# A graph network and mixture-of-experts kernel: late chunks of 31, 31 and 18 tiles instead of 18 and 30, and a new order around both ends of layer 2

## The chip, the cores and the metric

One core of one Trainium2 chip. The time is the device time of one execution in microseconds (us). The number to forecast is the median of the kernel's runs. Five engines work side by side: TensorE (PE, with its weight loads as PEld), VectorE (DVE), ScalarE (ACT), GpSimd (POOL) and SyncE (SP). SP, ACT and POOL also issue DMAs.

## What is computed

Two graph convolutions over 6250 nodes and 206250 weighted edges, sorted by destination, then a mixture of 8 experts, 2 chosen for each node. With rows of 256 features:

```python
norm = edge_weight * rsqrt(deg_out[src] * deg_in[dst] + EPS)
h6 = relu(segment_sum((LN(x) @ W6)[src] * norm, dst) + b6)
h7 = relu(segment_sum((h6 @ W7)[src] * norm, dst) + b7)
x = x + h7 @ Wp + bp
x = x + moe(LN(x))      # LN again, router, top 2 of 8, gelu(xn @ W1[e] + b1[e]) @ W2[e] + b2[e]
```

## The kernel before

**Two ways to sum the edges.** The sorted edges lie in tiles of 128, and 8 tiles are a group. There are 202 groups. The first edges are taken densely. A chunk of 30 or 31 tiles covers at most 128 destination rows, and for it a matrix of 128 columns by 49 x 128 source rows is built once, in layer 1. DVE makes two one-hots for a tile (`tile_one_hots`), PE multiplies them (`build_tile`, three bf16 matmuls), and DVE adds the product to the chunk's matrix in `adj` (`add_tile`). PE then multiplies the 49 blocks of the matrix with the node table in `xp` (`apply_step`; 49 blocks in 27 steps). The finished matrix is stored to `chunks` in HBM, and layer 2 only loads it (`load_chunk`, seven DMAs on ACT's queue) and applies it. The other edges are taken sparsely: POOL gathers the source rows of a group from the table in HBM with eight indirect DMAs (`gathers`), PE sums them with 16 short matmuls (`sums`) and joins every two groups (`combine`), ACT copies the result out (`copy_rows`), and SP stores it to `zsum`. Four buffers hold gathered groups (`RING`): POOL may start on a group when PE has summed the one four before.

**Layer 1** has 24 dense chunks (736 tiles) and 110 groups. The first 96 groups run beside the chunks in a loop over tiles. The last 14 (`TAIL`) have a turn each, numbered k = 0 to 13. In turns 0 to 3 PE applies the last chunk. In all of them late tiles (`EXTRAS`) are built into two further chunks, 24 and 25, of 18 and 30 tiles, which only layer 2 applies: it has 26 chunks (784 tiles), and so 104 groups. From turn 4 on the pairs 9 to 22 go through (`TAIL_PAIRS`). A pair is 256 destination rows: SP loads its sums (`load_early`), DVE scales them, PE turns them, ACT applies the relu, PE projects with W7, ACT copies out and SP stores the rows to table 1 (`store_table`). In the last turn pair 23 is projected ahead of the sums of the last group; pair 24 (the last) follows behind the last group. Chunk 24 is stored by ACT at turn 5, layer 2's chunk 0 is loaded by ACT at turn 7 into the buffer that chunk 24 left, and chunk 25 is stored by SP behind the last pair. Layer 2's gathers wait on POOL until all 25 pairs are in table 1 (`p_stored`).

**Layer 2** runs in slots, one group in each, as every engine's `layer2_slot`. A chunk spans 3 slots (chunks 0 to 7) or 4 (8 to 25), so the chunks end with slot 95 (`CHUNKS_END` = 96). A pair goes through six stages in six slots from the slot where it starts (`pair_starts`; at least three slots between starts). Stage 0 loads, scales and turns. In stage 1 PE projects with Wp and DVE adds the residual and computes two norms (`residual_and_norms`). Stage 2 is the router, stage 3 the ranks and places, stages 4 and 5 the lists of rows by expert. Pairs 0 to 10 need dense sums only, pair 11 is the merged one, and 12 to 24 need groups. At slot 96 ACT waits for the last chunk and issues 16 weight loads (`load_experts`). At slot 99 DVE works out the table of whole blocks (`list_whole`), and at slot 101 it copies the list and the first rows (`copy_list`, `block_rows`). From slot 104 on two expert blocks of 128 rows take the place of a group. Slots 104 to 112 still hold stages of the last pairs; after them come 87 blocks alone, of 105.

Before layer 1, a set-up of some 360 us computes degrees, features and bounds.

The plans follow from the constants. Starts of pairs before, as (slot, pair): (10, 0) (13, 12) (16, 1) (20, 13) (23, 2) (30, 14) (33, 3) (38, 15) (41, 4) (46, 16) (49, 5) (54, 17) (57, 6) (62, 18) (65, 7) (70, 19) (73, 8) (78, 20) (85, 9) (88, 21) (93, 10) (96, 22) (99, 11) (104, 23) (107, 24).

Of the kernel before, what the change touches and what calls it, by code (L numbers as in the profile page):

```python
# [34 lines left out]
LATE_CT, SHORT = (18, 30), 8  # L35
# [3 lines left out]
SPANS = [3] * SHORT + [4] * (ALL - SHORT)  # L39
# [7 lines left out]
MERGED_PAIRS = 11,  # L47
# [6 lines left out]
PARTS_OUT = 16  # L54
PIECE = 7

OFFS, CHUNK_OFFS = 16, 32

# [27 lines left out]
def gnn_moe_kernel(nc, A):  # L86
# [37 lines left out]
    with ExitStack() as ctx:  # L124
# [83 lines left out]
        SC_W = 5 * DTX  # L208
# [344 lines left out]

        LAST_STEPS = [STEPS * k // TAIL_FROM for k in range(TAIL_FROM + 1)] + [STEPS] * (TAIL - TAIL_FROM)
# [20 lines left out]
        def group_no(L, n):  # L575
# [28 lines left out]
        def chunks_for(b):  # L604
            return next(c for c in range(ALL) if chunk_start(c) >= tiles_before((b + 1) * PT * P) + CT // 2)

        def groups_for(L, b):
            return min(2 * ceil_div(tiles_before((b + 1) * PT * P) + (2 * TG if L else TG) - G0[L] * TG, 2 * TG),
                       GROUPS[L])

        LATE_PAIR = LOOP_PAIRS + 1
        TURNS = TAIL - TAIL_FROM - 2
        TAIL_PAIR_COUNT = LATE_PAIR - EARLY_PAIRS
        TAIL_PAIRS = [range(0)] * TAIL_FROM + [range(EARLY_PAIRS + TAIL_PAIR_COUNT * k // TURNS,
                                                     EARLY_PAIRS + TAIL_PAIR_COUNT * (k + 1) // TURNS)
                                               for k in range(TURNS)] + [range(LATE_PAIR, NPAIR - 1), range(0)]
        assert LATE_PAIR == NPAIR - 2 and groups_for(0, LATE_PAIR) == GROUPS[0] - 2

# [70 lines left out]
        def _(sp):  # L689
# [141 lines left out]
            with sp.If(bad < 1):  # L831
# [39 lines left out]
                for k in range(TAIL):  # L871
# [5 lines left out]
                    if k == TAIL - 1:  # L877
                        store_table(LATE_PAIR)
                    if k % 2 == 0:
                        store_group(0, LOOP_GROUPS + k)  # L880
                    for b in TAIL_PAIRS[k]:
                        if b == LATE_PAIR:
                            load_early(b)
# [4 lines left out]
                        if k % 2 and b == TAIL_PAIRS[k][0]:  # L888
                            store_group(0, LOOP_GROUPS + k)
                    if k % 2 and not TAIL_PAIRS[k]:  # L890
                        store_group(0, LOOP_GROUPS + k)
                load_early(NPAIR - 1)
                store_table(NPAIR - 1)
# [3 lines left out]
                carry_chunk(1, 0)  # L897
                sp.wait_ge(added, DTA)
# [3 lines left out]
                def layer2_slot(n, c, j, g, stages):  # L902
                    for i, b, s in stages:
                        if s:
                            continue
                        if b in DENSE_PAIRS:
                            sp.wait_ge(zd_stored[1], 16 * chunks_for(b))
                        else:
                            sp.wait_ge(z_stored[1], 16 * (ZERO_FILLS[1] + min(n, GROUPS[1]) // 2))
                            if b in MERGED_PAIRS:  # L910
                                sp.wait_ge(zd_stored[1], 16 * ALL)
# [153 lines left out]
        def _(dve):  # L1065
# [601 lines left out]
            with dve.If(bad < 1):  # L1667
# [39 lines left out]
                tail_pair(NPAIR - 1)  # L1707
# [43 lines left out]
        def _(act):  # L1751
# [81 lines left out]
            def tail_pairs(pairs, n):  # L1833
                for b in pairs[:1]:
                    pair_root(b)
                for b in pairs:
# [5 lines left out]
                    if b == pairs[0]:  # L1842
                        copy_rows(0, n)
# [687 lines left out]
```

## Time and profile before

| | us |
|---|---|
| median of 3 runs | 3113.17 |
| lowest, highest | 3110.77, 3113.7 |
| the profiled execution | 3122.37 |
| its span, first to last instruction | 3120.4 |

| engine | busy us | share |
|---|---|---|
| PE | 2610.7 | 84% |
| DVE | 1911.7 | 61% |
| ACT | 861.9 | 28% |
| POOL | 1959.3 | 63% |

### The profile page before, as it was taken

What the parts mean: (1) busy time and instruction counts of PE and PEld (TensorE: products, weight loads), DVE (VectorE), ACT (ScalarE), POOL (GpSimd) and SP (SyncE); (2) the same over time, 40 slices, a digit from 0 to 9 for tenths busy, and PEclk for the clock granted to TensorE, in tenths of its full rate; (3) what the DMA queues carried; (4) which work ended last, traced back from release to release, by engine and by line L of the source; (5) the groups of instructions that cost most, each with busy time, mean ns of one, the idle gap of its engine ahead of it and who ended that gap; (6) DMA issues with size and microseconds to landing.
All of it is one profiled execution on the core that took longest, in us unless ns stands there. A gap on an engine that the chain in (4) does not pass through costs nothing. (4 is left out here: it accounts for less than half of the span.)

```text
span 3120.4 us, 54057 instructions
## 1 busy us (share of the span) xinstructions
PE 2610.7 (84%) x16919; PEld 2002.9 (64%) x16919; DVE 1911.7 (61%) x6029; ACT 861.9 (28%) x2052; POOL 1959.3 (63%) x1932
## 2 busy tenths in 40 slices
PE   4567479999999999996679989988888875899995
PEld 3456346676766766664457766666666653789984
DVE  9999878888878878784402554555555447632210
ACT  6677711211121221111200110111110001456652
POOL 0000177777777777777477777777777774467763
PEclk8699789999999999997889999989999986999998
DMA  4001345666555666656676776776676764344444
GB/s 134 0 22 44 107 152 197 202 203 205 183 177 201 204 205 203 195 196 223 186 240 221 253 242 222 229 229 228 216 229 217 238 204 146 62 69 71 70 69 115
DMA packets 222273, 531.08 MB, mean 170 GB/s; under 512 B 42345, under 2 KB 132510, under 8 KB 218814
## 3 DMA queue, kind: packets, MB, share of 16 engines
q0 software_dynamic: 102336, 252.47, 30.5%
q1 hardware_dynamic: 90158, 176.24, 15.9%
q10 hardware_dynamic: 29520, 99.17, 8.6%
q8 instruction: 131, 2.15, 0.3%
q14 instruction: 128, 1.05, 0.1%
HBM read 377.61 MB, written 156.51 MB: 171 GB/s over the span
## 5 line engine op out<-in xcount | busy, mean ns | idle before, releaser
L993 POOL DMA_INDIRECT arena<-table,src_i x1712 | 1676.4, 979 | 564.0 <-issue 518.4
L2135 PE MATMUL bank<-arena 128*128 128x257 f32 x4900 | 1248.9, 392 | 1.9 <-ACT zcd L1800 0.8
L2135 PEld LDWEIGHTS bank<-arena 128*128 128x128 f32 x4900 | 911.4, 196 | 187.8 <-issue 64.1
L1339 DVE TENSOR_TENSOR arena<-arena,bank 128x294 f32 x784 | 357.5, 456 | 179.4 <-PE bank L2120 166.5
L2120 PE MATMUL bank<-arena 128*128 128x294 bf16 x2352 | 423.9, 293 | 51.8 <-DVE arena L1311 32.3
L1311 DVE SCALAR_TENSOR_TENSOR arena<-iota_f,arena 128x256 f32<-128x256 f32 x784 | 367.0, 468 | 0.0
L2120 PEld LDWEIGHTS bank<-arena 128*128 128x128 bf16 x2352 | 225.5, 99 | 209.4 <-DVE arena L1339 50.6
L2148 PE MATMUL bank<-arena,s_all 128*32 128x257 f32 x3424 | 251.6, 415 | 83.3 <-DMA arena<-table,src_i 68.5
L1787 ACT COPY arena<-zero 128x2144 f32<-128x2144 f32 (+1 forms) x104 | 156.3, 1533 | 403.0 <-DMA chunks<-arena 321.5
L1019 POOL DMA_INDIRECT acc<-arena x105 | 173.9, 1657 | 131.9 <-ACT arena L1923 105.4
L1310 DVE TENSOR_SCALAR arena<-iota_key,arena 128x294 bf16<-128x294 bf16 x784 | 243.4, 310 | 0.0
L2092 PE MATMUL bank<-arena 128*128 128x150 bf16 x1616 | 151.7, 255 | 109.4 <-DVE arena L1159 73.6
L1599 DVE COPY arena<-arena 128x1024 f32 x105 | 76.3, 738 | 250.3 <-PE bank L2340 235.4
L984 POOL PARTITION_ALL_REDUCE bad_all<-bad_f x1 | 0.4, 380 | 359.5 <-DVE bad_f L1301 359.5
L2092 PEld LDWEIGHTS bank<-arena 128*128 128x128 bf16 x1616 | 131.9, 109 | 130.6 <-DVE arena L1159 109.2
L2148 PEld LDWEIGHTS bank<-arena,s_all 128*32 128x32 f32 x3424 | 94.4, 115 | 180.4 <-DMA arena<-table,src_i 75.3
L2340 PE MATMUL bank<-arena 128*128 128x128 f32 x1680 | 207.3, 277 | 0.0
L2349 PE MATMUL bank<-arena 128*128 x840 | 200.5, 380 | 6.2 <-ACT arena L1923 6.2
L1776 ACT COPY zs<-bank 127x257 f32<-127x257 f32 x107 | 40.1, 375 | 575.6 <-PE bank L2148 541.6
L2340 PEld LDWEIGHTS bank<-arena 128*128 128x128 f32 x1680 | 198.6, 194 | 0.1
L2349 PEld LDWEIGHTS bank<-arena 128*128 128x128 f32 x840 | 151.5, 190 | 25.0 <-issue 7.7
L1006 POOL DMA_INDIRECT arena<-rows_x,arena x105 | 107.2, 1021 | 70.3 <-issue 28.3
(238 smaller groups left out, 2643.0 us busy)
## 6 DMA issues: line engine op xcount, KB each, us to landing
arena<-chunks ACTq DMA_DIRECT2D x182, 469.0 KB
chunks<-arena SPq DMA_DIRECT2D x24, 3283.0 KB
arena<-table,src_i POOLq DMA_INDIRECT x1712
zsum<-zc SPq DMA_DIRECT2D x107, 128.5 KB
zrow<-zsum SPq DMA_DIRECT2D x50, 257.0 KB, 3.4
arena<-in_W ACTq DMA_DIRECT2D x16, 512.0 KB, 16.6
rows_x<-arena SPq DMA_DIRECT2D x25, 264.0 KB
zsum<-zcd SPq DMA_DIRECT2D x50, 128.5 KB, 3.3
```

The source lines that it names most:

```text
L993: pool.indirect_dma_start(gat[:, r, j, 0:D], None, table[L], bass.IndirectOffsetOnAxis(ap=src_i[:, col:col + 1], axis=0)).then_inc(gathere ...
L1019: pool.indirect_dma_start(acc, bass.IndirectOffsetOnAxis(ap=row_e[:, j:j + 1], axis=0), ye[:, j % 2], None, compute_op=ALU.add).then_inc(y ...
L1310: dve.tensor_scalar(ohk[:, r], iota_key[:, 0:KEYS], key[:, t:t + 1], None, ALU.is_equal)
L1311: dve.scalar_tensor_tensor(out=words[:, r], in0=bc_mid(iota_f[:, :], 2), scalar=lo_f[:, t:t + 1], in1=bc_in(w_words[:, t], P), op0=ALU.is_ ...
L1339: dve.tensor_tensor(win, win, ps_b[t % len(ps_b)].rearrange("p (h w) -> p h w", w=TW), ALU.add).then_inc(added, 1)
L1787: done = act.copy(adj[:, c % 2, first:first + whole], zero[:, :].unsqueeze(2).broadcast_to([P, whole, AWID]))
L2092: last = pe.matmul(ps_do, oh_lo[:, r, j // TI, :, j % TI], whi[:, r, j // TI, :, :, j % TI].rearrange("p i n -> p (i n)"), start=False, st ...
L2120: last = pe.matmul(ps_b[t % len(ps_b)], halves[:, t % OH_RING, word, :, half], ohk[:, t % OH_RING], start=(i == 0), stop=(i == 2))
L2135: last = pe.matmul(ps_ap, adj[:, c % 2, h, 0:P], xp[:, h], start=(h == 0), stop=(h == XB_ALL - 1))
L2148: last = pe.matmul(ps_seg[q * WIN:(q + 1) * WIN, :], s_mat[:, r, q * HQ + j], gat[:, r, q * HQ + j], start=(j == 0 and not second), stop=( ...
L2340: last = pe.matmul(ps_h[j % 2][:, c], w1_e[:, j % W1_RING, k, c * P:(c + 1) * P], xeT[:, j % 2, k], start=(k == 0), stop=(k == KD - 1))
L2349: last = pe.matmul(ps_y, hs[:, j % 2, c], w2_of(e, c), start=(c == 0), stop=(c == HC - 1))
```

## The change

- **Late chunks.** Three of 31, 31 and 18 tiles (80) instead of two of 18 and 30 (48). Layer 2 has 27 chunks and 100 groups instead of 26 and 104; layer 1 keeps 24 and 110. The new tiles are built in turns 0 to 12: 7, 8, 8, 8 | 6, 6, 6, 6, 7 | 4, 5, 4, 5, where they were 4, 5, 4, 5 | 3, 4, 4, 4, 3, 4, 4, 4.
- **Stores and loads around them.** ACT stores chunk 24 at turn 5 and chunk 25 at turn 10, and clears the buffer for chunk 26 at turn 8. Chunk 26 is stored by SP behind the last pair. Layer 2's chunk 0 goes to the other buffer (`(c + L) % 2`) and is loaded at turn 12.
- **Order of the tail.** PE combines after both pairs of a turn instead of between them, and ACT and SP copy and store after them. Pairs 23 and 24 both follow behind the last group.
- **Spans.** 14 chunks span 3 slots, spread over the layer, and 13 span 4; the chunks end with slot 93.
- **Starts of pairs in layer 2.** `chunks_for` asks for 3 tiles of margin instead of 15, group pairs but the last three start one slot later than their groups allow, and SP then waits only for the groups that the pair needs. The merged pair is 12 instead of 11 and starts at slot 99. The starts are (10, 0) (16, 1) (19, 13) (23, 2) (27, 14) (30, 3) (35, 15) (38, 4) (43, 16) (46, 5) (51, 17) (55, 6) (59, 18) (62, 7) (67, 19) (70, 8) (75, 20) (78, 9) (84, 10) (87, 21) (91, 11) (94, 22) (99, 12) (102, 23) (105, 24).
- **The end.** `list_whole` at slot 97, `copy_list` at 99, expert blocks from slot 100, 22 of them in the 11 slots to 110.
- **Weights.** Two experts' weights (four DMAs) at the ends of slots 93, 94, 95 and 96, behind the wait for the last chunk at the first.
- **Memory.** `SC_W` is the larger of what layer 1 and layer 2 need, instead of five times the dense tiles.

```diff
-LATE_CT, SHORT = (18, 30), 8
+LATE_CT, SHORT = (31, 31, 18), 5
-SPANS = [3] * SHORT + [4] * (ALL - SHORT)
+SPANS = [3 if c < SHORT or c % 5 in (0, 2) else 4 for c in range(ALL)]
-MERGED_PAIRS = 11,
+MERGED_PAIRS = 12,
+ROW_TILES = 3
+EXPERTS_EACH = 2
-        SC_W = 5 * DTX
+        SC_W = max(4 * DTX, 2 * DTX + E8, L2_WORDS)
...
-        EXTRAS = [range(DT + LATE_CT[0] * k // FIRST_EXTRA, DT + LATE_CT[0] * (k + 1) // FIRST_EXTRA)
-                  for k in range(FIRST_EXTRA)]
-        EXTRAS += [range(DT + LATE_CT[0] + LATE_CT[1] * k // 8, DT + LATE_CT[0] + LATE_CT[1] * (k + 1) // 8)
-                   for k in range(8)]
+        LATE_TURNS = FIRST_EXTRA, 5, 4
+        EXTRAS = [range(chunk_start(CHUNKS + i) + LATE_CT[i] * k // n, chunk_start(CHUNKS + i) + LATE_CT[i] * (k + 1) // n)
+                  for i, n in enumerate(LATE_TURNS) for k in range(n)]
-        FIRST_STORED_AT, FIRST_LOADED_AT = FIRST_EXTRA + 1, FIRST_EXTRA + 3
+        STORED_AT = FIRST_EXTRA + 1, sum(LATE_TURNS[:2]) + 1
+        ZEROED_AT, FIRST_LOADED_AT = sum(LATE_TURNS[:2]) - 1, TAIL - 2
...
-            return next(c for c in range(ALL) if chunk_start(c) >= tiles_before((b + 1) * PT * P) + CT // 2)
+            return next(c for c in range(ALL) if chunk_start(c) >= tiles_before((b + 1) * PT * P) + ROW_TILES)
-            return CHUNKS_END + 2 if b in MERGED_PAIRS else groups_for(1, b)
+            return CHUNKS_END + 5 if b in MERGED_PAIRS else groups_for(1, b) + (b in GROUP_PAIRS[:-3])
...
 SP, the tail of layer 1
-                    if k == TAIL - 1:
-                        store_table(LATE_PAIR)
...
-                load_early(NPAIR - 1)
-                store_table(NPAIR - 1)
+                    store_group(0, LOOP_GROUPS + k)
+                for b in range(LATE_PAIR, NPAIR):
+                    load_early(b)
+                for b in range(LATE_PAIR - 1, NPAIR):
+                    store_table(b)
...
 ACT, layer 2
-                if n == CHUNKS_END:
-                    load_experts()
+                if n == CHUNKS_END - 1:
+                    act.wait_ge(applied[1], SLICES * ALL)
+                if CHUNKS_END <= n + 1 < CHUNKS_END + NE // EXPERTS_EACH:
+                    e = (n + 1 - CHUNKS_END) * EXPERTS_EACH
+                    load_weights(range(e, e + EXPERTS_EACH))
...
 ACT, the tail of layer 1
+                    if k in STORED_AT:
+                        c = CHUNKS + STORED_AT.index(k)
+                        act.wait_ge(added, chunk_start(c + 1))
+                        for rows, part in chunk_pieces(c, c % 2):
+                            act.dma_start(rows, part).then_inc(chunk_stored, 16)
+                    if k == ZEROED_AT:
+                        act.wait_ge(chunk_stored, stores_until(CHUNKS + 1))
+                        for i in range(SLICES):
+                            zero_chunk(ALL - 1, *slice_bounds(i))
...
 PE, the tail of layer 1
-                    if k == TAIL - 1:
-                        project(LATE_PAIR, 0, w7, ps_f(LATE_PAIR))
                     sums(0, n)
...
-                    for b in TAIL_PAIRS[k][:1]:
+                    for b in TAIL_PAIRS[k]:
                         tail_pair(b)
                     combine(0, n)
-                    for b in TAIL_PAIRS[k][1:]:
-                        tail_pair(b)
-                pair_T(0, NPAIR - 1, (NPAIR - 1) % 2)
+                for b in range(LATE_PAIR, NPAIR):
+                    tail_pair(b)
```

## Rows read from the trace of the kernel before

**Rows 1.** Costliest groups of the page: busy us, mean ns; and a DMA issue group.
```profile
L993 POOL DMA_INDIRECT arena<-table,src_i x1712 | 1676.4, 979 | 564.0 <-issue 518.4
L2135 PE MATMUL bank<-arena 128*128 128x257 f32 x4900 | 1248.9, 392 | 1.9 <-ACT zcd L1800 0.8
...
L1787 ACT COPY arena<-zero 128x2144 f32<-128x2144 f32 (+1 forms) x104 | 156.3, 1533 | 403.0 <-DMA chunks<-arena 321.5
...
arena<-in_W ACTq DMA_DIRECT2D x16, 512.0 KB, 16.6
```
**Rows 2.** Windows: length, busy us by engine, PEclk, DMA share, GB/s.
```profile
1395.00:1475.00 80.00, 54.75 (x307) 36.57 (x311) 35.28 (x109) 11.06 (x21) 60.80 (x64) 0.76 0.72 244
...
1681.00:2551.00 870.00, 778.73 (x4576) 593.27 (x4580) 453.20 (x2001) 89.02 (x233) 659.62 (x691) 0.95 0.69 223
2551.00:2646.00 95.00, 42.98 (x235) 22.64 (x227) 60.35 (x282) 8.28 (x22) 52.47 (x55) 0.59 0.60 201
2646.00:2744.00 98.00, 85.13 (x553) 75.41 (x553) 58.88 (x247) 48.94 (x141) 44.72 (x33) 0.94 0.35 68
2744.00:3096.00 352.00, 330.52 (x2268) 303.27 (x2268) 71.99 (x153) 201.16 (x608) 230.72 (x171) 0.99 0.41 66
```
**Rows 3.** Timeline of POOL: last gather of layer 1, first and last of layer 2.
```profile
1523.25 0.95 POOL L993 DMA_INDIRECT arena<-table,src_i  x1 [0.30 <-issue]
1564.23 0.94 POOL L993 DMA_INDIRECT arena<-table,src_i  x1 [40.03 <-DMA table<-arena]
...
2611.46 0.95 POOL L993 DMA_INDIRECT arena<-table,src_i  x1 [0.30 <-issue]
```
**Rows 4.** Timeline of PE: sums of groups 10, 96 and 101, a run of dense matmuls.
```profile
1681.01 1.94 PE L2148 MATMUL bank<-arena,s_all 128*32 128x257 f32 x16 [5.14 <-issue]
...
2026.61 3.64 PE L2135 MATMUL bank<-arena 128*128 128x257 f32 x16
...
2550.57 1.08 PE L2148 MATMUL bank<-arena,s_all 128*32 128x257 f32 x16
...
2614.88 1.94 PE L2148 MATMUL bank<-arena,s_all 128*32 128x257 f32 x16 [6.49 <-issue]
```
**Rows 5.** Waits of PE, two from 1681 to 2551, three from 2551 to 2646.
```profile
PE bank L2200 <- DVE arena L1135: 37.7, 19, 3.0
PE bank L2161 <- DMA zs<-zsum: 10.6, 3, 4.0
...
PE bank L2200 <- DVE arena L1135: 13.7, 1, 13.7
PE bank L2231 <- ACT arena L1862: 13.2, 2, 12.8
PE bank L2235 <- DVE arena L1486: 10.3, 1, 10.3
```
**Rows 6.** Timeline of ACT, PE and DVE in the tail of layer 1.
```profile
1451.86 4.41 ACTq L2037 DMA_DIRECT2D chunks<-arena  x7
...
1469.37 0.20 ACT L1815 ACTIVATE din<-din 128x2 f32<-128x2 f32 x1 [12.86 <-DVE din L1369]
...
1476.41 1.84 PE L2120 MATMUL bank<-arena 128*128 128x294 bf16 x12
...
1502.41 0.45 DVE L1339 TENSOR_TENSOR arena<-arena,bank 128x294 f32 x1
...
1503.38 0.46 DVE L1339 TENSOR_TENSOR arena<-arena,bank 128x294 f32 x1
```
**Rows 7.** Timeline of PE: sums of layer 1's last two groups.
```profile
1532.70 1.68 PE L2148 MATMUL bank<-arena,s_all 128*32 128x257 f32 x16
...
1545.56 1.94 PE L2148 MATMUL bank<-arena,s_all 128*32 128x257 f32 x16
```
**Rows 8.** Timeline of PE: first expert block, and blocks 18 and 19.
```profile
2646.13 0.66 PE L2330 MATMUL bank<-ident,arena 128*128 128x128 f32 x2 [0.51 <-issue]
...
2744.50 1.95 PE L2340 MATMUL bank<-arena 128*128 128x128 f32 x16
...
2748.24 1.95 PE L2340 MATMUL bank<-arena 128*128 128x128 f32 x16
```

More of the change, by code:

```diff
@@ L54 @@
 PARTS_OUT = 16
+EXPERTS_EACH = 2
 PIECE = 7
 OFFS, CHUNK_OFFS = 16, 32
+L2_WORDS = 3640
 TINY_EW = 2.0 ** -15
@@ L551, in slice_bounds @@
             return first_of_step(ZERO_BEHIND[i - 1] + 1) if i else 0, first_of_step(ZERO_BEHIND[i] + 1)
+        LATE_PAIR = LOOP_PAIRS + 1
+        TURNS = TAIL - TAIL_FROM - 2
+        TAIL_PAIR_COUNT = LATE_PAIR - EARLY_PAIRS
+        TAIL_PAIRS = [range(0)] * TAIL_FROM + [range(EARLY_PAIRS + TAIL_PAIR_COUNT * k // TURNS,
+                                                     EARLY_PAIRS + TAIL_PAIR_COUNT * (k + 1) // TURNS)
+                                               for k in range(TURNS)] + [range(0)] * 2
         LAST_STEPS = [STEPS * k // TAIL_FROM for k in range(TAIL_FROM + 1)] + [STEPS] * (TAIL - TAIL_FROM)
@@ L604, in chunks_for @@
         def chunks_for(b):
-            return next(c for c in range(ALL) if chunk_start(c) >= tiles_before((b + 1) * PT * P) + CT // 2)
+            return next(c for c in range(ALL) if chunk_start(c) >= tiles_before((b + 1) * PT * P) + ROW_TILES)
         def groups_for(L, b):
[L608 to L617, printed above, removed]
+            return min(2 * ceil_div(tiles_before((b + 1) * PT * P) + 2 * TG - G0[L] * TG, 2 * TG), GROUPS[L])
         PAIR_IN_CHUNK = {chunks_for(b) + 1: b for b in range(EARLY_PAIRS)}
@@ L1831, in pair_out, with tail_pairs @@
                 last.then_inc(p_out, 1)
-            def tail_pairs(pairs, n):
+            def tail_pairs(pairs):
                 for b in pairs[:1]:
@@ L1841, in tail_pairs @@
                         pair_out(b - 1)
-                    if b == pairs[0]:
-                        copy_rows(0, n)
-                if not pairs:
-                    copy_rows(0, n)
             def features_T(i):
@@ L1932, in load_chunk @@
             def load_chunk(c):
-                for rows, part in chunk_pieces(c, c % 2):
+                for rows, part in chunk_pieces(c, (c + 1) % 2):
                     act.dma_start(part, rows).then_inc(chunk_in[c % 2], 16)
             def load_first(c):
-                act.wait_ge(chunk_stored, stores_until(CHUNKS + c + 1))
+                act.wait_ge(chunk_stored, stores_until(CHUNKS + c + 2))
                 load_chunk(c)
@@ L2065, in _ @@
                 act.wait_ge(p_stored, 16 * NPAIR)
-                load_weights()
+                load_weights(range(NE))
                 with act.Fori(0, NPAIR) as b:
@@ L2134, in apply_step @@
                         pe.wait_ge(chunk_carried, 16 * (L * CHUNKS + c + 1))
-                    last = pe.matmul(ps_ap, adj[:, c % 2, h, 0:P], xp[:, h], start=(h == 0), stop=(h == XB_ALL - 1))
+                    last = pe.matmul(ps_ap, adj[:, (c + L) % 2, h, 0:P], xp[:, h], start=(h == 0), stop=(h == XB_ALL - 1))
                 if step in ZERO_BEHIND:
```

37 lines of the change are left out of this document (12 added, 25 removed).

## The prediction

> **What bounds the kernel now.** I read the page's costliest groups first. POOL's indirect gathers of layer 1 and 2 are the largest group, 1676 us of a 3120 us span [rows 1], and the obvious reading is that fewer gathers mean a shorter kernel. So the next question is whether anybody waits for them. The table of windows cuts the span at its stages: 870 us in which layer 2 runs dense chunks and gathers side by side (slots 10 to 95), 95 us of its last eight slots, 98 us of nine slots that mix expert blocks with the last pairs, and the experts alone [rows 2]. POOL issues without a pause inside layer 2: from 1564.23 to 2611.46 lie 832 gathers, 1.26 us each, 10.08 us a group [rows 3]. But PE is busy 779 of the 870 us [rows 2], and the waits of PE in that stretch name DVE, ACT and a carry row, and no gather [rows 5]. PE takes up group 10 at 1681.0 and group 96 at 2550.6 [rows 4]: 869.6 us for 86 slots, 10.11 each, against POOL's 10.08. The two engines run level, PE seven us behind at group 10 (whose last gather went out at 1674) and ten at group 96, with four gather buffers between them. Taking work from POOL and giving it to PE is then no gain by itself. At both ends of layer 2 it is neither: POOL stands still from 1524 to 1564 [rows 3] because table 1 isn't complete, and after its last gather at 2611 PE needs 35 us until the first expert block, in a stretch where the granted clock is 0.59 [rows 2].
>
> **The change, part by part,** against the profiled run's own 3122.4 us, which is 9.2 above the median of the three runs shown; the same 9.2 are taken off at the end.
>
> *Layer 2, gathers.* 104 groups become 100: 32 gathers, 32 x 1.26 = 40 us of POOL. On the path this is worth nothing unless PE keeps up.
>
> *Layer 2, one more dense chunk.* 49 steps are 98 matmul rows (4900 rows for 50 chunks) [rows 1]. Sixteen of them take 3.64 us, the last one's own 0.38 included, so 0.217 each [rows 4], and the chunk 21.3 us, or 22.4 at this stretch's clock of 0.95. Two groups fewer in slots 10 to 93 take off 2 x 1.25 (16 sum rows at about 1 us, half a combine) = 2.5. The work fills gaps: PE waits 37.7 us in 19 places for DVE's norms [rows 5], about 2 us each, because the norm chain outlasts the slot; the mean slot grows from 7.3 to 7.8 steps, which is 0.35 us, twice per pair, so some 6 us of that wait go. Sum: 22.4 - 2.5 - 6 = +14. Lower bound -3 (the gaps take it all in, the two groups are saved), upper bound +25 (nothing is filled and one more of the 4 us carry waits comes with the chunk). PE then needs 884 us from slot 10 to slot 94, where POOL needs 84 x 10.08 = 847: PE falls from 7 to over 30 us behind, the ring is full and POOL stands. PE is the bound.
>
> *Group pairs a slot later.* The load of a pair no longer waits on SP for the group stored just before, and SP's carry row behind it comes earlier. PE waited 10.6 us for carry rows, in three places, up to 4.0 [rows 5]. I take -3 (0 to -11). The mixed spans move work between slots and leave the sum.
>
> *The end of layer 2.* Before, all 16 weight loads of 512 KB [rows 1] are issued at slot 96. PE then waits 12.8 us for an ACT copy that stands behind them in ACT's order, 13.7 for the norms whose input was late, and 10.3 for the list copy after the long list arithmetic [rows 5]. The eight slots take 95.5 us, 2550.6 to 2646.1 [rows 4, 8]. After, six slots remain, four loads are issued in each of slots 93 to 96, and the merged pair starts in slot 99, so that its norms fall into expert slots. Slots 94 to 98 hold what 96 to 100 held, which took 64 us, 2550.6 to 2614.9 [rows 4]; minus 9 for the ACT copy and 4 for the norm's late input gives 51. The last slot holds the list copy and the first row copies, about 13. Together 64 against 95.5: -31. Bounds -42 (no transfer is late at all) and -15 (only ACT's issue time goes). The trace shows that bytes and not only issues count: a root on ACT waited 12.9 us for a pair row while a chunk store, whose seven issues took 4.4 us, was landing [rows 6]. The Trainium skill (DMA: Bandwidth & Descriptors, Issuing engines are not separate DMA queues) says the same of issue: all transfers interleave on the same engines, and another way of issuing saves only sequencer time; by it alone this term would stand near its -15 end.
>
> *The merged pair among the experts.* Eighteen blocks and two pairs take 98.2 us, 2646.1 to 2744.3; a block alone takes 3.74 [rows 8]. 98.2 - 67.4 leaves 31 for two pairs and the start; I take 12 for a third (7, its bare matmuls, to 16).
>
> *The tail of layer 1.* 32 more dense tiles in the 14 turns. PE builds four in 1.84 us, 0.46 each, when they are ready, but DVE adds one per 0.97 us [rows 6], and only three are built ahead, so a tile costs 0.46 to 0.97 on PE's path. The 13 added in turns 0 to 3 lie between dense steps, 13 x 0.46 = 6; I take 4, since PE is busy only 55 of the 80 us around them [rows 2]. The 3 of turn 4 hide behind a row load, 2 of turn 5 in its wait of 12.9 [rows 6]. Eight in turns 6 to 8 cost 8, one in turn 10 costs 1. ACT's zeroing, four copies at 1.53 [rows 1], lies beside the tiles of turn 8: +1. The chunk load of turn 7 goes from ACT's order there (-5), and the new store in turn 10 costs 4.4 of issue [rows 6] and some 3 of slower loads: +7. Sum: +16 at turn 12. In the older order pair 23 no longer stands between turns 12 and 13, which are 12.9 us apart now [rows 7]: five tiles and the sums need 5 to 6, so -7; but pair 23 now stands in front of pair 24 behind the last group: +5. With +2 for the chunk load beside these small transfers the start of layer 2 moves by +16. Bounds: -5 (the tiles fill waits, and only the order counts) and +40 (below).
>
> *Set-up.* One more span in the bounds: six or so short DVE instructions, +1.
>
> Sum: 1 + 16 + 14 - 3 - 31 + 12 = +9. 3122.4 + 9 = 3131 on the profile's scale, **3122** on that of the median.
>
> **The rivals.** *POOL's pace comes through (faster).* If PE's gaps take in the new chunk and cold stretches vanish, slot 94 comes at POOL's 847 us after slot 10, not 884: -37 against the forecast, and 3122 - 37 = 3085. For it: 96 us of waits in 870 and a granted clock of 0.95 [rows 2]: after a wait of 5.1 us the sixteen sum rows of a group took 1.94 us, otherwise 1.08 [rows 4]. A mean of 0.95 is a tenth of the time at the lower level, so 43 us to win. Against it: the waits come from DVE's chain, whose length the change leaves. The Trainium skill (TensorE: Matmul & The Clock Gate, HAM oscillation — how this bites in real kernels) says that gaps of waiting put the array back to the lower clock and that denser work avoids it; by it the time would be this rival's 3085. Half of the rival's effect gives 3103. Chance 0.28.
>
> *Layer 1's tail becomes the bound (slower).* The place is turns 5 to 12, where PE is already some 20 us behind POOL (turn 12's sums at 1532.7 [rows 7], its last gather at 1513 by POOL's pace). If a tile costs its full 0.97 (31 us), the second store brings back turn 5's wait of 12.9, and only the order gives back 2, turn 12 comes over 40 us later. It decides once a turn's sums are over 30 us behind, four buffers' worth: then POOL stands as well. Start of layer 2 +40 instead of +16: 3146. Speaking against: turns have 2 us waits that tiles can use. Chance 0.17.
>
> *The change does less than it says.* The chunk is hidden by half, weights still collide with gathers, and both ends cancel: within 6 us of 3113. Chance 0.12.
>
> **How the numbers follow.** The forecast has 0.43 and its own range is 3106 to 3140. The range for 8 in 10 reaches from the first rival's time to the second's: 3085 to 3147; what is left out is what lies beyond either, where several terms stand at the same end of their bounds. A measurement of this kernel can tell about 0.2%, 6.2 us, from no change. Faster by more: the first rival and the lower edge of the forecast, 0.32. Within: the third rival and a part of the forecast, 0.21. Slower: 0.47.
>
> **What would show it.** Right: POOL's gathers of layer 2 show idle time released by PE's sums, absent now; the last sums of layer 1 to the first gather of layer 2 stay near 19 to 24 us, but POOL's restart lies near 1580, not 1564; slot 94's sums come about 1000 us after the restart; from there to the first expert block about 64 us, with no 12.8 us wait for ACT's copy; the first 22 blocks take about 125 us. Wrong: a POOL without such idle time and a restart near 1565 speak for the first rival; a restart past 1595 for the second. What would spoil the sum most is that PE's gaps in layer 2 are worth more or less than the 6 us that I took.

## The result and the profile after

The changed kernel takes 3129.53 us (median of 5 runs, 3127.19 to 3132.53), the kernel before 3113.17 (median of 5, 3110.77 to 3119.86). The ratio is 1.0045, 95% interval 1.0023 to 1.0067: slower by 0.45%. The forecast was 3122 with a range of 3085 to 3147, and slower was the likeliest of the three signs. The profiled run of after took 3129.11 us (span 3127.3), so it lies on its median, where that of before lay 9.2 above. The ratios are of fast runs; one run of all those reported here was a slow one, 5306 us, and it counts in its kernel's median of ten (the first experiment on the order of the tail).

The costliest groups of the page, to compare with [rows 1]:

```profile
L989 POOL DMA_INDIRECT arena<-table,src_i x1680 | 1650.4, 982 | 576.0 <-issue 508.0
L2130 PE MATMUL bank<-arena 128*128 128x257 f32 x4998 | 1262.2, 390 | 2.7 <-ACT zcd L1797 1.9
...
arena<-in_W ACTq DMA_DIRECT2D x16, 512.0 KB, 5.9
```

32 gathers fewer, 98 matmul rows more, and a weight load lands 5.9 us after its issue instead of 16.6. POOL's timeline, the last gather of layer 1, the first of layer 2, and the first and last of its last group [rows 3]:

```profile
1522.16 0.94 POOL L989 DMA_INDIRECT arena<-table,src_i  x1 [0.30 <-issue]
1576.53 0.94 POOL L989 DMA_INDIRECT arena<-table,src_i  x1 [53.42 <-DMA table<-arena]
...
2588.32 0.95 POOL L989 DMA_INDIRECT arena<-table,src_i  x1 [6.27 <-PE bank L2143]
2597.13 0.95 POOL L989 DMA_INDIRECT arena<-table,src_i  x1 [0.30 <-issue]
```

POOL leaves layer 1 a microsecond earlier than before and starts layer 2 12.3 us later. PE's timeline: the sums of groups 10 and 94, and the sums of the last two groups of layer 1 with the wait behind them [rows 4, 7]:

```profile
1544.16 1.08 PE L2143 MATMUL bank<-arena,s_all 128*32 128x257 f32 x16
...
1546.03 1.08 PE L2143 MATMUL bank<-arena,s_all 128*32 128x257 f32 x16
1556.41 1.20 PE L2156 MATMUL bank<-zs,arena 128*128 128x257 f32 x2 [9.30 <-DMA zs<-zsum]
...
1692.91 1.70 PE L2143 MATMUL bank<-arena,s_all 128*32 128x257 f32 x16 [3.51 <-issue]
...
2570.63 1.08 PE L2143 MATMUL bank<-arena,s_all 128*32 128x257 f32 x16
```

Windows: the middle of layer 2, its last six slots, 22 blocks with three pairs [rows 2]:

```profile
1694.00:2571.00 877.00, 793.98 (x4632) 611.84 (x4628) 448.54 (x1995) 88.83 (x232) 664.14 (x690) 0.95 0.69 225
2571.00:2638.00 67.00, 30.28 (x172) 15.30 (x161) 42.21 (x195) 5.60 (x15) 20.00 (x21) 0.60 0.65 212
2638.00:2764.00 126.00, 108.19 (x695) 96.48 (x695) 79.31 (x337) 60.42 (x174) 57.22 (x43) 0.93 0.34 67
```

Waits (total us, times, longest): of POOL from 1576 to 2640, of PE from 1694 to 2571, and the three longest of PE from 2571 to 2638 [rows 5]:

```profile
POOL arena L989 <- PE bank L2143: 10.3, 6, 6.3
...
PE bank L2195 <- DVE arena L1131: 35.5, 16, 4.1
PE bank L2244 <- DVE off_i L1472: 21.4, 20, 1.5
PE bank L2165 <- DVE zr_all L1374: 13.4, 6, 5.3
...
PE bank L2195 <- DVE arena L1131: 9.3, 1, 9.3
PE bank L2165 <- DVE next_of L1463: 8.6, 1, 8.6
PE bank L2143 <- issue: 7.9, 1, 7.9
```

POOL now waits for PE's sums, where the same row of before had 0.9 us in three places. The carry row's waits of this stretch (10.6 us) are gone, as is the wait of 12.8 us for ACT's copy at the end. The norms still cost PE 35.5 us, where 37.7 stood, and in the last slots one wait for norms of 9.3 is now the longest. The 13.4 us are for a pair's scaled rows, for which PE waited 3.8 before:

```profile
PE bank L2170 <- DVE zr_all L1378: 3.8, 4, 1.4
```

So most of what went at the carry rows came back there. All of PE's waits in this stretch together went from 96.4 to 83.0 us.

**The account of the two profiled runs.** Start of layer 2 +12.3 (1564.2 to 1576.5). From there to the last sums with a chunk, slot 96 before and 94 after, 986.3 and 994.1: +7.8. On to the first expert block (2637.4) 95.6 and 66.8: -28.8. Then 22 blocks in 113.3 and 126.4: +13.1. What is left, 360.9 and 363.5: +2.6. Sum +7.0; the spans differ by 6.9. But the medians are 16.4 apart, and the other 9 have to be found too. That was the first thing that the experiments settled.

### The profile page after: what moved, and what is told of

The parts are those of the page before. It is cut to its first block and busy times, and to the rows that moved or that the text cites. A ratio compares the mean times of both kernels' runs of the same rounds, so it can differ in the third digit from the quotient of the medians.

```text
span 3127.3 us, 54466 instructions
## 1 busy us (share of the span) xinstructions
PE 2628.4 (84%) x17045; PEld 2024.8 (65%) x17045; DVE 1934.4 (62%) x6119; ACT 867.8 (28%) x2055; POOL 1938.5 (62%) x1900
## 5 line engine op out<-in xcount | busy, mean ns | idle before, releaser
L989 POOL DMA_INDIRECT arena<-table,src_i x1680 | 1650.4, 982 | 576.0 <-issue 508.0
L2130 PE MATMUL bank<-arena 128*128 128x257 f32 x4998 | 1262.2, 390 | 2.7 <-ACT zcd L1797 1.9
L2130 PEld LDWEIGHTS bank<-arena 128*128 128x128 f32 x4998 | 924.7, 194 | 188.1 <-issue 63.3
L2115 PE MATMUL bank<-arena 128*128 128x294 bf16 x2448 | 443.2, 295 | 56.3 <-DVE arena L1307 32.6
L1335 DVE TENSOR_TENSOR arena<-arena,bank 128x294 f32 x816 | 370.9, 455 | 186.1 <-PE bank L2115 172.0
L1307 DVE SCALAR_TENSOR_TENSOR arena<-iota_f,arena 128x256 f32<-128x256 f32 x816 | 382.1, 468 | 0.0
L2115 PEld LDWEIGHTS bank<-arena 128*128 128x128 bf16 x2448 | 234.7, 100 | 222.8 <-DVE arena L1335 60.0
L2143 PE MATMUL bank<-arena,s_all 128*32 128x257 f32 x3360 | 242.3, 408 | 90.2 <-DMA arena<-table,src_i 65.7
L2087 PEld LDWEIGHTS bank<-arena 128*128 128x128 bf16 x1616 | 130.3, 108 | 131.5 <-DVE arena L1155 110.0
L2335 PEld LDWEIGHTS bank<-arena 128*128 128x128 f32 x1680 | 201.2, 196 | 0.1
L2344 PEld LDWEIGHTS bank<-arena 128*128 128x128 f32 x840 | 151.8, 191 | 26.5 <-issue 9.2
## 6 DMA issues: line engine op xcount, KB each, us to landing
zsum<-zc SPq DMA_DIRECT2D x105, 128.5 KB, 3.4
```

What stands on the lines that cost most here:

```text
L989: pool.indirect_dma_start(gat[:, r, j, 0:D], None, table[L], bass.IndirectOffsetOnAxis(ap=src_i[:, col:col + 1], axis=0)).then_inc(gathere ...
L1307: dve.scalar_tensor_tensor(out=words[:, r], in0=bc_mid(iota_f[:, :], 2), scalar=lo_f[:, t:t + 1], in1=bc_in(w_words[:, t], P), op0=ALU.is_ ...
L1335: dve.tensor_tensor(win, win, ps_b[t % len(ps_b)].rearrange("p (h w) -> p h w", w=TW), ALU.add).then_inc(added, 1)
L2087: last = pe.matmul(ps_do, oh_lo[:, r, j // TI, :, j % TI], whi[:, r, j // TI, :, :, j % TI].rearrange("p i n -> p (i n)"), start=False, st ...
L2115: last = pe.matmul(ps_b[t % len(ps_b)], halves[:, t % OH_RING, word, :, half], ohk[:, t % OH_RING], start=(i == 0), stop=(i == 2))
L2130: last = pe.matmul(ps_ap, adj[:, (c + L) % 2, h, 0:P], xp[:, h], start=(h == 0), stop=(h == XB_ALL - 1))
```

## The experiments

Each has runs of the kernel before beside it on the same chip in the same hour. There were three hours, each on another chip, and their medians were 3121.66 (25 runs), 3114.93 (31) and 3112.32 (17), so the ratio counts and not the time, and two ratios of different hours are also of different chips. Each trace is also a further look at the stages that its edit leaves alone.

### Where the missing 9 us are: the starts of layer 2

Five of the experiments below keep the tail of layer 1 as it was before. POOL's first gather of layer 2 in each, from its timeline: with the weights alone, the new starts of pairs, a chunk's matmuls left out, gathers left out, the merged pair late.

```profile
1555.87 0.94 POOL L993 DMA_INDIRECT arena<-table,src_i  x1 [35.13 <-DMA table<-arena]
```
```profile
1554.28 0.94 POOL L994 DMA_INDIRECT arena<-table,src_i  x1 [30.54 <-DMA table<-arena]
```
```profile
1553.94 0.95 POOL L993 DMA_INDIRECT arena<-table,src_i  x1 [30.22 <-DMA table<-arena]
```
```profile
1552.34 0.95 POOL L994 DMA_INDIRECT arena<-table,src_i  x1 [32.20 <-DMA table<-arena]
```
```profile
1556.09 0.95 POOL L993 DMA_INDIRECT arena<-table,src_i  x1 [34.91 <-DMA table<-arena]
```

They lie at 1552 to 1556, median 1554.3; the profiled run of before lies at 1564.2 [rows 3], and its turn 12 at 1532.7 [rows 7] where these five have 1519.1 to 1523.6. So the 9.2 us by which it was above its median can be placed in the tail of layer 1, the part that the change rebuilds. Four kernels with the changed tail start at 1572.2, 1576.5, 1576.9 and 1581.4, median 1576.7. So the tail costs 22 us, not the 12 that the two profiled runs show. Then the account is 22.4 + 7.8 - 28.8 + 13.1 + 2.6 = +17.1, and the medians say +16.4, or 7 to 21 by the interval. Only the first term is a median of traces, the others are of one trace each, so the good fit is partly luck. From the start of layer 2 on, the changed kernel's profiled run is 5 us faster; it loses 22 ahead of it.

Turn 12's sums come at 1540.2 to 1549.1 in the four, median 1544.0, against 1520.0: +24. From there to the start it is 31.9 to 33.1 us in the four and 32.3 to 35.2 in the five. So all of it is in turns 0 to 12, and the end of the tail costs nothing net.

### What the order of the tail costs

**Combine between pairs again.** The changed kernel, where PE combines after the first pair of a turn and ACT and SP copy and store there, as before. Pairs 23 and 24 stay behind the last group.

```diff
-                    for b in TAIL_PAIRS[k]:
+                    for b in TAIL_PAIRS[k][:1]:
                         tail_pair(b)
                     combine(0, n)
+                    for b in TAIL_PAIRS[k][1:]:
+                        tail_pair(b)
```

> The changed kernel with one part undone: in the tail of layer 1 PE combines between the two pairs of a turn, and ACT and SP copy, store and carry there, as before the change; pairs 23 and 24 still follow behind the last group. My theory: the wait of 9.3 us for the carry row ahead of the last combine goes, because the store of turn 11 is out before the load of layer 2's chunk 0; POOL restarts 6 to 10 us earlier after the same last sums, and the kernel is 5 to 10 us faster than the changed one, near 3120 to 3124. Rival: the load's bytes delay whatever small transfer runs beside them, so the wait only moves to the next store; within 3 us of the changed kernel.

Measured: 3120.69, ratio 1.0016 (0.9995 to 1.0036), start of layer 2 at 1568.5. The changed kernel has 1.0045 (1.0023 to 1.0067). By the ratios it is some 9 us better, by the start 8, but the intervals overlap. The wait for the carry row, which my theory had gone, is still there with 6.69 us. Of the 8 us, 5 stood already in turn 12's sums (1539.1 against 1544.2); from there to the start it took 29.4 us instead of 32.4.

**Chunk 0 loaded behind the last pair.** In the changed kernel the 9.30 us wait lies beside the load of layer 2's chunk 0, seven DMAs of 469 KB that ACT issues at 1544.3 to 1549.

```diff
-                    if k == FIRST_LOADED_AT:
-                        load_first(0)
...
                 pair_out(NPAIR - 1)
+                load_first(0)
                 load_first(1)
```

> The changed kernel, with layer 2's chunk 0 loaded by ACT behind the last pair instead of at turn 12. Theory: the 9.30 us for which PE waits at the last combine are the group store and the carry row lying beside this 3.3 MB load; without the load there the wait falls to 2 to 5 us and POOL starts layer 2 near 1570 instead of 1576.5. The load lands some 16 us after the last pair, while POOL gathers the first group and PE waits anyway (16.3 us), so nothing is lost behind: 4 to 7 us faster than the changed kernel, 3122 to 3126. Rival (the wait is the round trip of a store and a load behind two table stores, whatever else moves): the wait stays 7 to 9 us, and the time stays at 3129 or goes up by the late chunk.

Measured: 3128.74, ratio 1.0062 (1.0043 to 1.0082). The same combine in its timeline:

```profile
1547.87 1.20 PE L2155 MATMUL bank<-zs,arena 128*128 128x257 f32 x2 [3.98 <-DMA zs<-zsum]
```

The wait fell from 9.30 to 3.98, and the other three kernels with the tail of the changed one have 9.1 to 9.7, so the wait grows with the load beside it. Little of the gain comes through. Layer 2 starts at 1571.2, 5.3 earlier, but turn 12's sums were 3.2 earlier already (1540.9), which is scatter; from there to the start it took 30.3 us instead of 32.4. The last store to table 1, now beside the same load, was issued 4.66 us ahead of POOL's first gather, where it is 2.04 in the changed kernel. The median shows no gain.

**The whole order of before,** with the combine between pairs and pair 23 ahead of the last group's sums, on the changed kernel. Of its edit only the part for pair 23 is shown.

```diff
+                    if k == TAIL - 1:
+                        project(LATE_PAIR, 0, w7, ps_f(LATE_PAIR))
                     sums(0, n)
...
-                for b in range(LATE_PAIR, NPAIR):
-                    tail_pair(b)
+                pair_T(0, NPAIR - 1, (NPAIR - 1) % 2)
```

> The changed kernel with the whole order of the kernel before in the tail of layer 1: PE combines between pairs, and pair 23 goes through ahead of the last group's sums, so that only pair 24 follows behind it. The chunks of 31, 31 and 18 tiles, their stores and the load of chunk 0 at turn 12 stay. The traces so far put the start of layer 2 (POOL's first gather) at 1552 to 1556 in four of five traces with the tail of before and at 1572 to 1581 with the changed tail; with the combine alone between pairs it was 1568.5. Theory (12 us come from the added tiles and the second store, 9 from the order and the carry wait): start near 1567, 8 to 12 us faster than the changed kernel, 3118 to 3122. Rival (the tiles cost next to nothing and the order is all): start near 1558, 17 to 20 faster, 3110 to 3113.

Measured: 3128.86, ratio 1.0058 (1.0036 to 1.0080), start at 1577.8: no gain at all, against both theories. Its timeline of PE in turn 12:

```profile
1542.01 1.89 PE L2195 MATMUL bank<-w,hT 128*128 128x256 f32 x8
1554.52 1.12 PE L2178 MATMUL bank<-ident,zr_all 128*128 128x128 f32 x4 [10.62 <-DVE zr_all L1382]
```

Here it is pair 23 whose row load lies beside the load of chunk 0: a wait of 10.62 in the place of the 9.30 for the carry row. In these kernels whatever small transfer stood beside that load paid.

**Both.** The two edits together.

```diff
-                    if k == FIRST_LOADED_AT:
-                        load_first(0)
...
+                    if k == TAIL - 1:
+                        project(LATE_PAIR, 0, w7, ps_f(LATE_PAIR))
```

> Both: the order of before in the tail and chunk 0 loaded behind the last pair. Theory: start of layer 2 near 1562, some 14 us faster than the changed kernel, about 3115, level with the kernel before. If the two share the same wait, it is no better than the order alone (3118 to 3122).

Measured: 3127.44, ratio 1.0054 (1.0033 to 1.0074), start at 1576.8. The wait for pair 23 fell to 3.66, but its turn 12 came at 1543.1, and from there to the start it took 33.7. That is the tail of before behind turn 12, and still 22 us later. So the order was not the cost; what is common to all these kernels is the 32 added tiles, the second store and the clearing of the buffer behind it. No run takes one of the three away alone. Why the combine between pairs alone came out 8 us earlier stays open.

### What the end of layer 2 gains

**The weights alone,** on the kernel before.

```diff
-                if n == CHUNKS_END:
-                    load_experts()
...
+                if n == CHUNKS_END - 1:
+                    act.wait_ge(applied[1], SLICES * ALL)
+                if CHUNKS_END <= n + 1 < CHUNKS_END + NE // 2:
+                    load_weights(range(2 * (n + 1 - CHUNKS_END), 2 * (n + 1 - CHUNKS_END) + 2))
```

> The kernel before with one part of the change alone: the weights are loaded two experts at a time, at the ends of slots 95 to 98, instead of all at slot 96. My theory: ACT's queue no longer holds up the copies of the pairs behind 16 issues, so the 12.8 us wait of PE for an ACT copy at 2566 goes, and with it part of the 13.7 us wait for the norms; the 95.5 us from the sums of group 96 to the first expert block become 80 to 86, and the kernel is 9 to 15 us faster (ratio 0.995 to 0.997). Rival: the bytes hold the pairs up, not the issues; then the stretch stays over 90 us and the kernel within 5 us of before.

Measured: 3113.9 against 3121.66, ratio 0.9973 (0.9958 to 0.9988), the only kernel with all of the work that is clearly faster than before. Its last eight slots, and what PE waits for in them:

```profile
2541.00:2627.00 86.00, 43.81 (x240) 23.18 (x237) 61.66 (x284) 8.30 (x22) 53.51 (x57) 0.60 0.70 225
...
PE bank L2198 <- DVE arena L1135: 9.6, 1, 9.6
PE bank L2168 <- DVE next_of L1467: 8.4, 1, 8.4
...
PE bank L2229 <- ACT arena L1862: 0.9, 2, 0.5
```

95.6 us became 86.1, the upper edge of what was expected, and the ratio lies just above its range. Of the 12.8 us for ACT's copy 0.5 is left and of the 13.7 for the norms 9.6, but the list copy kept its wait (10.6, before 10.3), and one of 8.4 for another result of DVE (`next_of`) is there where 1.4 stood.

**The merged pair where it was,** in the changed kernel: it starts at slot 97 instead of 99.

```diff
-            return CHUNKS_END + 5 if b in MERGED_PAIRS else ...
+            return CHUNKS_END + 2 if b in MERGED_PAIRS else ...
```

> The changed kernel with the merged pair 12 started three slots earlier than planned there (plan slot 96, so it starts at 97, pair 23 at 100, pair 24 at 103; experts from slot 100 in 9 slots of pairs instead of 11). My theory: its norms and router stand in slots 98 and 99, which then take 12 to 20 us more before the first block, and the mixed slots lose one pair, 11 to 13 us: within 7 us of the changed kernel, rather slower. Rival: the slots before the experts have room (PE waits there anyway), so it is 8 to 12 us faster.

Measured: 3132.11, ratio 1.0052 (1.0029 to 1.0074). From slot 94's sums to the first block's second stage it took 78.7 us instead of 69.2, and the first 22 blocks 119.0 instead of 124.0. So the later place gives 9.5 (8.1 if one counts to the first block's first stage) and takes 5 back among the blocks; what is left is too little for the median to show. The wait that the earlier place brings back among PE's in 2572 to 2649 is the one for the list copy, 0.7 in the changed kernel; the wait of 9.3 for norms is there with either place:

```profile
PE bank L2230 <- DVE arena L1482: 9.8, 1, 9.8
PE bank L2195 <- DVE arena L1131: 9.3, 1, 9.3
```

**The merged pair late, on the kernel before with the weights.**

```diff
-            return CHUNKS_END + 2 if b in MERGED_PAIRS else groups_for(1, b)
+            return CHUNKS_END + 5 if b in MERGED_PAIRS else groups_for(1, b)
```

> The kernel before with two parts of the change: the weights two experts a slot, and the merged pair 11 started at slot 101 instead of 99, so that its router and lists fall among the expert blocks. Against the first part alone: the wait for the list copy behind the norms shortens, but one pair's stages 3 to 5 move among the experts, 3 to 6 us. I expect within 6 us of the kernel with the weights alone. Rival: starting it later frees 10 us or more before the first block, and it is 5 to 10 us faster than the weights alone.

Measured: 3115.72 against 3114.93, ratio 0.9995 (0.9980 to 1.0010), where the weights alone had 0.9973: no gain, and perhaps a loss (the intervals overlap). From slot 96's sums to the first block it took 88.4 us instead of 86.1. In eight slots instead of six the later place doesn't take the pair's norms out of the stretch. PE's waits from 2539 to 2632 have two of them where the weights alone had one, of 9.6:

```profile
PE bank L2198 <- DVE arena L1135: 20.0, 2, 10.3
```

The wait for the list copy (10.6) is down to 0.7 here too: one wait went and one for norms came.

**The new starts of pairs,** on the kernel before with the weights: group pairs a slot later, SP's shorter waits, three tiles of margin.

```diff
-            ... >= tiles_before((b + 1) * PT * P) + CT // 2)
+            ... >= tiles_before((b + 1) * PT * P) + 3)
...
-            return CHUNKS_END + 2 if b in MERGED_PAIRS else groups_for(1, b)
+            return CHUNKS_END + 2 if b in MERGED_PAIRS else groups_for(1, b) + (b in GROUP_PAIRS[:-3])
```

> The kernel before with two experts' weights a slot and with the changed starts of pairs alone: group pairs but the last three a slot later, SP waiting only for the groups that a pair needs, three tiles of margin for dense pairs; merged pair, chunks and tail as before. The kernel with the weights alone had a ratio of 0.9973 to before. Theory (the later pairs take away the 10.6 us that PE waits for carry rows): 0 to 5 us better than that, ratio 0.9955 to 0.9975. Rival (the wait for carry rows is covered by PE's distance behind POOL and the later pairs only shift work towards the end): ratio 0.9975 to 1.000.

Measured: 3108.32 against 3112.32, ratio 0.9986 (0.9962 to 1.0010), not better than the weights alone. PE's waits from 1670 to 2544:

```profile
PE bank L2199 <- DVE arena L1136: 32.7, 14, 3.6
PE bank L2160 <- DMA zs<-zsum: 22.7, 5, 7.3
```

The waits for carry rows went up, from 9.1 us in three places with the weights alone to 22.7 in five. My reason for this part was wrong. That the changed kernel shows none of them may come from its distance behind POOL: up to slot 94 PE takes up a group as much as 32 us after its last gather (group 72), in the kernel before 24.5 (group 26), so a row has more time to come in. No run shows this by itself.

### Which engine layer 2 waits for

**32 gathers left out,** in the kernel before and in the changed one: half the gathers of eight groups of layer 2, 40 us of POOL. PE sums what lies in the buffers, so its work stays.

```diff
+    LESS = range(8, 96, 11)
...
-                for j in range(TG):
+                for j in range(TG // 2 if L == 1 and n in LESS else TG):
```

> The kernel before with 32 gathers of layer 2 left out (half the gathers of 8 groups, spread over slots 8 to 85; their sums then read old rows, so the output is not the reference's). It takes the change's 40 us of POOL away and adds nothing to PE. My theory: PE sets the pace of layer 2, so the kernel gains 0 to 10 us, and only PE's lag behind POOL grows. Rival (POOL sets the pace): 30 to 40 us faster.

> The changed kernel with 32 gathers of layer 2 left out (half the gathers of 8 groups; their sums then read old rows, so the output is not the reference's). My theory: PE is the bound of layer 2 here, so 0 to 5 us faster than the changed kernel. Rival (POOL's pace still counts): 20 us or more.

Measured: before 3101.77 (4 runs), ratio 0.9930 (0.9908 to 0.9951); after 3125.7, ratio 1.0035 (1.0021 to 1.0049) against 1.0045. POOL's waits for PE in layer 2, before, then after:

```profile
POOL arena L994 <- PE bank L2150: 31.1, 14, 4.9
```
```profile
POOL arena L990 <- PE bank L2145: 56.3, 24, 7.3
```

In the kernel before, 40 us less on POOL brought its last gather 12 us nearer to the first (1035.6 instead of 1047.2), and the rest became waiting for PE. Slot 96's sums came 977.4 us after the start of layer 2, where three kernels with the same layer 2 have 982.8 to 986.3, and from the start to the end of the program the trace is 6 us shorter. The time fell by 20, of which 11 to 14 I can't place. In the changed kernel the waits rose from 10.3 to 56.3, so POOL doesn't date its layer 2. Slot 94's sums came 990.8 us after the start against 994.1, and the ratio says 3 us too, but the six kernels with an unedited layer 2 of the changed kind scatter from 989.6 to 998.4 there.

**A chunk's matmuls left out,** again in both: 44 of the 49 blocks of chunk 13 in layer 2, 19 us of PE.

```diff
+                if L and c in (13,):
+                    blocks = blocks[-1:] if step in ZERO_BEHIND else blocks[:1] if step == 0 else blocks[:0]
```

> The kernel before with 44 of the 49 blocks of chunk 13 left out of PE's work in layer 2 (88 matmul rows, 19.1 us at 0.217 each; the output lacks them). My theory: PE and POOL run level in this kernel, so PE's gain of some 15 us meets POOL's pace (POOL needs 10.08 us a group, PE 10.11): 0 to 8 us faster. If PE alone were the bound: 14 to 19 us faster. If POOL alone: 0.

> The changed kernel with 44 of the 49 blocks of chunk 13 left out of PE's work in layer 2 (88 rows, 19.1 us; the output lacks them). My theory: here PE is the bound, with POOL 20 to 30 us ahead, so 10 to 17 us faster than the changed kernel, near 3114 to 3120. Rival (POOL's pace or fixed waits bound layer 2 here too): within 4 us of the changed kernel, near 3127.

Measured: before 3122.4, ratio 1.0006 (0.9993 to 1.0020); after 3131.1, ratio 1.0033 (1.0016 to 1.0050). Nearly nothing in either; for the changed kernel I had expected 10 to 17 us, and the rival came true. The windows of the four slots with chunk 13, in this order: before, before without the blocks, after, after without the blocks.

```profile
2037.00:2075.00 38.00, 36.64 (x207) 27.32 (x211) 17.31 (x76) 3.46 (x10) 28.86 (x31) 0.88 0.73 232
```
```profile
2031.00:2062.00 31.00, 19.65 (x119) 9.83 (x122) 13.15 (x56) 3.48 (x10) 23.39 (x25) 0.67 0.81 260
```
```profile
2047.00:2083.00 36.00, 33.74 (x216) 25.95 (x218) 16.93 (x81) 4.24 (x12) 27.16 (x30) 1.00 0.71 231
```
```profile
2039.00:2070.00 31.00, 18.85 (x132) 12.17 (x134) 17.97 (x84) 4.57 (x12) 23.38 (x26) 0.74 0.77 252
```

PE's busy time falls by 17.0 and 14.9 us, the stretch by 7 and 5. The granted clock goes from 0.88 to 0.67 and from 1.00 to 0.74, so what is left is dearer, and PE waits more. In the kernel before one wait of 6.6 us for a pair's scaled rows and one of 2.4 for a carry row have come. In the changed kernel it is the norms: 2.3 us with the blocks, without them

```profile
PE bank L2198 <- DVE arena L1131: 10.4, 1, 10.4
```

Of the 5 us, counted from the window's start, 3.8 are left at slot 48's sums and none at slot 94's; of the 7 in the kernel before 2 are left at slot 96's. Where they went the runs don't show. In the kernel before there was little to win: from POOL's start to slot 96's sums it took 986.3 us, and 96 groups at POOL's 10.08 and the 14.6 that the first group takes to reach PE are 982.3. In these slots the dense steps are work that PE does while DVE works out norms or scales rows. So neither POOL's pace nor PE's busy time alone dates the layer 2 of the changed kernel; that the waits for DVE's chains do is the likeliest reading, and no run tests it. The Trainium skill (TensorE: Matmul & The Clock Gate, HAM oscillation — how this bites in real kernels) says that gaps in the stream of matmuls send the array back to its lower clock; these windows agree. The test has a limit: blocks left out in four slots in a row tell what a local gap costs, not what the same time would bring spread over the layer.

## Why the prediction was right, and where its steps were off

Sign and range held; the time was 7.3 us too low. The forecast's steps in its own order, with the start of layer 2 from the medians of five and four traces and the other rows from the two profiled runs:

| step | forecast | measured |
|---|---|---|
| set-up and tail of layer 1 | +17 | +22.4 |
| chunk and pairs in layer 2 | +11 | +7.8 |
| last slots | -31 | -28.8 |
| merged pair among the blocks | +12 | +13.1 |
| remaining blocks | 0 | +2.6 |
| sum | +9 | +17 |

**The offset.** I took the 9.2 us between profile and median as common to both kernels and took them off at the end. They were not common: they lay in the very turns that the change rebuilds, and after's profiled run didn't have them. The stage times of [rows 6, 7] were therefore a dear sample, and read from them the tail seemed to cost 12. As the error of the tail's own size was on the other side, 3131 on the profile's scale against 3129.1 looks better than it is. Taking the 9.2 off did no harm to the sum itself, as it only leads back to the median of before; the 7.3 us are in the terms. That their errors partly cancel is luck.

**The tail** is the mis-sized term: +16 and +1 against +22.4. The mechanism is the one named. A tile beyond those built ahead costs PE the pace of DVE's add (PE, tail of after, turn 9, and its waits from 1450 to 1545):

```profile
1511.54 0.55 PE L2115 MATMUL bank<-arena 128*128 128x294 bf16 x3 [0.45 <-DVE arena L1335]
1512.51 0.55 PE L2115 MATMUL bank<-arena 128*128 128x294 bf16 x3 [0.42 <-DVE arena L1335]
...
PE bank L2115 <- DVE arena L1335: 7.1, 13, 1.8
```

0.97 us between two tiles, as taken. Median of the four kernels with the changed tail less median of the five with that of before, turn by turn, each at the turn's sums: +5.9 at turn 4 (forecast 4), +9.4 at turn 6, +15.6 at turn 9, +16.9 at turn 10, +22.8 at turn 11 and +24.0 at turn 12 (forecast 16). At turn 0 the two groups lie within each other's scatter (1394 to 1399 and 1390 to 1399). So turns 4 and 5 cost 3.5, where the tiles were to hide behind a row load at no cost; turns 6 to 8 cost 6.2 where 8 for the tiles, 1 for the clearing and -5 for the chunk load that left turn 7 made 4 (turn 7 to 8 was only 1.2 shorter); turn 10 cost 5.9 of its 8, and turns 9 and 11 over a microsecond each, for which I had nothing. Which part is the tiles' and which the second store's stays open.

The turns behind turn 12 came out at nothing net, as -7 + 5 + 2 said, but by another way. The last two groups' sums lie 1.9 us apart, where I had 5 to 6: only two tiles were left to build there. And 9.3 came from the carry row, which the load of chunk 0 held up, where I had given the load +2. So one sign of being right failed: from the last sums of layer 1 to the first gather of layer 2 it took 30.5 us, not 19 to 24.

**Layer 2.** PE is up to 32 us behind, POOL waits for its sums, and slot 94's sums came 994 us after the start where about 1000 stood. The six traces with the changed layer 2 have a median of 995.3, and three with that of before have 985.0 at slot 96: +10, nearer to the forecast's +11 than the two profiled runs. "PE is the bound" was right for the kernel after in that POOL waits for PE there, but 19 us of PE's work left out brought nothing, so it isn't PE's busy time that counts. For the kernel before it was too simple. There PE is only 4 us behind what POOL's pace allows at slot 96, POOL waits less than 1 us for it, and gathers left out brought slot 96's sums 8 to 9 us nearer. The first rival (3085) would have needed PE's waits and its clock to give way. The clock stayed at 0.95, and the waits fell by 13 us, 9 of which the forecast had taken, though as 6 at the norms, where it was 2.2, and 3 at the carry rows.

**The end.** The -31 for six slots held (-28.8). The spread of the weights gave 9.5 on the kernel before, the merged pair's place 8.1 in the changed kernel, and 11.2 are the remainder, which no run has by itself. The parts don't simply add: on the kernel before with the weights the later place made the stretch 2.3 longer. The forecast had 13 for the weights and 18 for the rest. Its reason for the merged pair, norms that fall into expert slots, is not what the runs show: the wait that the later place takes away is the list copy's, and one of 9.3 for norms stays. The Trainium skill (DMA: Bandwidth & Descriptors, Issuing engines are not separate DMA queues) says that another way of issuing saves only sequencer time; for the weights alone the trace agrees: 9.5 us is no more than their issue had held up (12.8).

**The rivals.** The second rival's mechanism, the tail as the bound, came true in part: the restart came at 1576.5, inside its fence of 1595, and there was no second wait of 12.9 us for the new store. That the change does less than it says was not seen: each part shows in the trace.

## What to carry to other kernels

A profiled run that lies above its median isn't slow everywhere: before its rows serve as prices for the stage that a change rebuilds, look at that stage in a second trace. Where two engines run level, leave work out on each side in turn; here 40 us less on POOL brought slot 96 some 8 us nearer in the one kernel and nothing clear of scatter in the other, and 19 less on PE gave next to nothing in either, which no busy share tells. Here a large load beside a chain of small transfers delayed whichever was next, and another order of the chain or a later load mostly changed which one that was.

## What was not expected of the hardware

A carry row was issued 8.1 us after the store of 128.5 KB that it waited for (1546.81 and 1554.92) while chunk 0 was being loaded; with that load put off it was 2.9 (1543.59 and 1546.45), and the page's median for the landing of such a store is 3.4. Taking 19.1 us of matmuls away (by the price of a row) lowered the granted clock of the stretch by 0.21 and 0.26, and PE's busy time fell by 17.0 and 14.9. And runs of one kernel scatter by some 10 us on either side of their median (3103.36 to 3125.63 in one hour). In the traces part of that lies in the unedited tail of layer 1: its turn 12 came between 1519.1 and 1532.7.
